# Moving list numbers and two blocks of gate products to GpSimd, and one block of one-hots to VectorE, in a two-phase attention and product-key expert kernel

## The reference

```python
q = (x @ Wq + bq).reshape(B, S, 8, 64)              # 8 heads
s1 = einsum(q[..., :32], K1); s2 = einsum(q[..., 32:], K2)   # 64 scores each
v1, i1 = top_k(s1, 10); v2, i2 = top_k(s2, 10)
all_scores = v1[..., :, None] + v2[..., None, :]
all_indices = i1[..., :, None] * 64 + i2[..., None, :]
vals, best = top_k(all_scores, 10)                   # 80 (head, place) slots a token
expert_idx = take_along_axis(all_indices, best)
h = gelu(einsum(x, W_down[expert_idx])) * softmax(vals)
out = einsum(h, W_up[expert_idx])
```

## Time and profile before

| what | value |
|---|---|
| time before, median of 3 | 3576.75 us (3570.31 to 3582.39) |
| the profiled execution's own time | 3578.76 us |
| its span from first to last instruction | 3577.0 us |
| PE busy | 89% |
| DVE busy | 87% |
| ACT busy | 59% |
| POOL busy | 53% |
| mean granted clock of PE | 0.887 of full |

### The profile page before, as it was taken

One profiled execution on the slowest core, in us unless ns is written; L12 is line 12 of the kernel. 1 busy time (PEld: TensorE's weight loads), 2 busy tenths in 40 slices (PEclk: granted clock), 3 DMA queues, 4 the chain that ended last, 5 costly groups with the idle time before them and its releaser, 6 DMA issues. The chain is left out here.

```text
span 3577.0 us, 91251 instructions
## 1 busy us (share of the span) xinstructions
PE 3185.3 (89%) x31284; PEld 2739.2 (77%) x31284; DVE 3098.0 (87%) x15084; ACT 2120.2 (59%) x4411; POOL 1901.8 (53%) x1694
## 2 busy tenths in 40 slices
PE   5999999963599999999999999999999999999988
PEld 3666666642488888888888888888888888888878
DVE  5666666646999999999999999999999999999971
ACT  3444444422666666666666766666666666766662
POOL 1333333333466665556556666666555555666664
PEclk9999999985699889888888988998998888988988
DMA  2111111103333333333333333333333333333332
GB/s 64 48 54 54 54 54 53 42 30 135 137 118 119 112 105 119 116 105 105 105 105 120 124 119 118 118 106 104 126 110 105 105 105 113 124 123 117 113 115 96
DMA packets 132329, 356.85 MB, mean 100 GB/s; under 512 B 13866, under 2 KB 61610, under 8 KB 129453
## 3 DMA queue, kind: packets, MB, share of 16 engines
q1 hardware_dynamic: 131868, 351.03, 30.0%
HBM read 309.01 MB, written 25.17 MB: 93 GB/s over the span
## 5 line engine op out<-in xcount | busy, mean ns | idle before, releaser
L1196 PE MATMUL b_ps_a<-b_wup,b_hid 128*128 128x256 f32 x4096 | 955.8, 379 | 1.5 <-POOL b_hid L1020 1.5
L1185 PE MATMUL b_ps_h<-b_xT_hi,b_wd_split 128*128 128x256 f32 x4096 | 934.4, 312 | 21.3 <-ACT b_hid L1336 20.5
L1196 PEld LDWEIGHTS b_ps_a<-b_wup,b_hid 128*128 128x128 f32 x4096 | 744.3, 190 | 85.7 <-POOL b_hid L1020 1.7
L1020 POOL TENSOR_TENSOR b_hid<-b_hid,b_gates 128x512 f32<-128x512 f32 x512 | 662.2, 1296 | 228.8 <-ACT b_hid L1336 228.8
L1185 PEld LDWEIGHTS b_ps_h<-b_xT_hi,b_wd_split 128*128 128x128 f32 x4096 | 705.5, 201 | 37.0 <-issue 26.5
L1315 ACT ACTIVATE b_ohq<-b_q_no,b_minus_qid 80x128 f16<-80x128 f16 x2048 | 648.7, 391 | 1.0
L1110 PE MATMUL b_ps_s<-b_ohr,b_ohq 80*128 80x32 f16 x16384 | 452.9, 185 | 173.5 <-issue 132.2
L1001 POOL TENSOR_SCALAR b_rstd<-b_mv 128x2 f32<-128x2 f32 x64 | 140.6, 2197 | 870.6 <-DVE b_mv L1375 870.6
L1185 PE MATMUL b_ps_h<-b_xT_lo,b_wd_split 128*128 128x256 f32 x2048 | 597.8, 292 | 0.0
L1110 PEld LDWEIGHTS b_ps_s<-b_ohr,b_ohq 80*128 80x128 f16 x16384 | 444.2, 102 | 182.4 <-issue 138.9
L1336 ACT ACTIVATE b_hid<-b_ps_h 128x512 f32<-128x512 f32 x512 | 303.9, 594 | 373.0 <-PE b_ps_h L1185 372.9
(11 more groups left out here) (192 smaller groups left out, 5534.4 us busy)
## 6 DMA issues: line engine op xcount, KB each, us to landing
b_wd_split<-wd_parts SPq DMA_DIRECT2D x512, 512.0 KB, 3.8
a_keysh<-a_key SPq DMA_DIRECT2D x16, 896.0 KB, 5.4
a_x<-in_x SPq DMA_DIRECT2D x16, 512.0 KB, 5.0
x_between<-a_y SPq DMA_DIRECT2D x16, 512.0 KB, 3.2
b_x<-x_between SPq DMA_DIRECT2D x32, 256.0 KB, 2.8
wd_parts<-b_wd_split SPq DMA_DIRECT2D x16, 512.0 KB, 3.1
b_x1t<-x_between SPq DMA_DIRECT2D x32, 256.0 KB, 5.4
out<-b_y SPq DMA_DIRECT2D x32, 256.0 KB, 5.5
```

Source lines behind the costliest of these rows:

```text
L1020: G.tensor_tensor(hid[:, p % 4, :, :], hid[:, p % 4, :, :], gates[:, 2 * p:2 * p + 2, :], ALU.mult).then_inc(mix_done, 1)
L1185: mm = T.matmul(hbank[p % 2][:, j * C:(j + 1) * C], a, c, start=i == 0, stop=i == len(parts) - 1)
L1196: mm = T.matmul(abank[:, t * D:(t + 1) * D], hid[:, p % 4, j, t * P:(t + 1) * P], wup[:, 2 * p + j, :], start=p == 0 and j == 0 and t == 0 ...
```

## The change

Four things change together.

1. `numbers` is moved from DVE to POOL, ahead of `pair_numbers` at place 10.
2. POOL no longer makes block 0 of `ohq`. It multiplies blocks 0 and 1 of `ohr` by the high and low gates, 10 parts of 13 tokens at places 3 to 12 (AT_PARTS), two instructions a part with a wait between them. DVE makes the equality of both blocks in one instruction (`equal`), between `lists_first` and `lists_rest`.
3. ACT makes block 0 of `ohq` instead of block 1, and DVE makes blocks 1, 2 and 3. The factors for POOL's one-hots go from `decode`. `ohq` now has three buffers and `ohr` all four blocks; block 3 of `ohq` shares the buffer of block 0 and waits for PE to have read that one.
4. `low_gates` moves from place 5 to 3; the places found by the second top-k lie in the memory of `picked`; ACT's `r_numbers` and `negate` come ahead of the first gelu.

```diff
-POOL_PARTS = 13
+POOL_PARTS = 10
+AT_PARTS = 3
-AT_GLO, AT_CID = 5, 10
+AT_GLO, AT_CID = 3, 10
-    ohq = sb("b_ohq", [SLOTS, C, NQ], F16)
-    ohr = sb("b_ohr", [SLOTS, 2, BLK, 2, NR], F16)
+    ohq = sb("b_ohq", [SLOTS, 3, BLK, NQ], F16)
+    ohr = sb("b_ohr", [SLOTS, C, 2, NR], F16)
...
-        def onehots(m, p):
...
-            G.tensor_tensor(ohq[:, tok, :].rearrange("p n (a b) -> p n a b", a=16),
-                            oh16[:, tok, :].unsqueeze(3).to_broadcast(shape),
-                            oh8[:, tok, :].unsqueeze(2).to_broadcast(shape), ALU.mult).then_inc(ohq_pool_done, 1)
+        def onehots(m, i):
+            tok = slice(i * 13, min(i * 13 + 13, 2 * BLK))
+            shape = [SLOTS, tok.stop - tok.start, NR]
+            hi, lo = (ohr[:, tok, part, :] for part in range(2))
+            pool.wait_ge(equal_done, m + 1)
+            pool.wait_ge(glo_done, m + 1)
+            G.tensor_tensor(hi, lo, ghi[:, tok, 0:1].to_broadcast(shape), ALU.mult).then_inc(pool_hi_done, 1)
+            pool.wait_ge(pool_hi_done, POOL_PARTS * m + i + 1)
+            G.tensor_tensor(lo, lo, glo[:, tok, 0:1].to_broadcast(shape), ALU.mult).then_inc(pool_lo_done, 1)
...
+        def numbers(m):
+            i = idx[:, :, :, 0:TOPK].rearrange("p t (h s) k -> p h s k t", s=2)
+            pool.wait_ge(lists_done[0], 5 * (m + 1))
+            pool.wait_ge(lists_done[1], 5 * (m + 1))
+            if m:
+                pool.wait_ge(cid_done, m)
+            G.tensor_scalar(id1[:, :, :, :], i[:, :, 0, :, :], float(NSQ), -2048.0, ALU.mult, ALU.add)
+            G.tensor_scalar(id2[:, :, :, :], i[:, :, 1, :, :], 0.0, None, ALU.add).then_inc(ids_done, 1)
...
                 if p == AT_CID and has(m + 2):
+                    numbers(m + 2)
                     pair_numbers(m + 2)
-                if p < POOL_PARTS and has(m + 1):
-                    onehots(m + 1, p)
+                if p >= AT_PARTS and p < AT_PARTS + POOL_PARTS and has(m + 1):
+                    onehots(m + 1, p - AT_PARTS)
...
+        def equal(m):
+            shape = [SLOTS, 2 * BLK, NR // 2, 2]
+            dve.wait_ge(q_no_done, 1)
+            dve.wait_ge(rid_done, m + 1)
+            if m:
+                dve.wait_ge(gates_pe, GROUPS * m)
+            V.tensor_tensor(ohr[:, 0:2 * BLK, 1, :].rearrange("p n (r s) -> p n r s", s=2),
+                            rid[:, 0:2 * BLK, :].unsqueeze(2).to_broadcast(shape),
+                            q_no[0:SLOTS, 0:NR].rearrange("p (r s) -> p r s", s=2).unsqueeze(1).to_broadcast(shape),
+                            ALU.is_equal).then_inc(equal_done, 1)
...
             if has(m + 2):
                 lists_first(m + 2, 0)
+            if has(m + 1):
+                equal(m + 1)
...
-                numbers(m + 2)
                 pair_sums(m + 2)
...
-                onehots_r(m + 1, 0)
+                onehots_r(m + 1, 2)
             if has(m + 1):
-                onehots_r(m + 1, 1)
+                onehots_q(m + 1, 1)
                 onehots_q(m + 1, 2)
             if has(m):
                 finish(m)
             if has(m + 1):
-                onehots_q(m + 1, 3)
-                onehots_r(m + 1, 2)
+                onehots_r(m + 1, 3)
             if has(m):
                 norm_out(m)
             if has(m + 1):
-                onehots_r(m + 1, 3)
+                onehots_q(m + 1, 3)
```

More of the change, by code:

```diff
@@ L826, in experts_phase @@
     idx = sb("b_idx", [P, NT, LISTS, 16], U16)
-    top, pos = val[:, 0, :, :], idx[:, 0, :, :]
+    top = val[:, 0, :, :]
     id1 = sb("b_id1", [P, HEADS, TOPK, NT], F16)
@@ L878, in experts_phase @@
     half_set, xT_lo_done, wd_lo_done, mix_done, res_done = (sem(f"b_{n}") for n in ("half", "xT_lo", "wd_lo", "mix", "res"))
-    ohq_pool_done, cid_done, glo_done = (sem(f"b_{n}") for n in ("ohq_pool", "cid", "glo"))
+    pool_hi_done, pool_lo_done, cid_done, glo_done = (sem(f"b_{n}") for n in ("pool_hi", "pool_lo", "cid", "glo"))
     eps_done = [sem(f"b_eps{i}") for i in range(2)]
@@ L889, in experts_phase @@
     shift_done, gsum_done, grecip_done, gate_done = (sem(f"b_{n}") for n in ("shift", "gsum", "grecip", "gate"))
-    q_no_done, eid_done, fields_done, qid_done, id16_done, oh16_done = (
-        sem(f"b_{n}") for n in ("q_no", "eid", "fields", "qid", "id16", "oh16"))
+    q_no_done, eid_done, fields_done, qid_done, equal_done = (
+        sem(f"b_{n}") for n in ("q_no", "eid", "fields", "qid", "equal"))
     ohr_eq_done, ohr_hi_done, ohr_lo_done, ohq_done = (sem(f"b_{n}") for n in ("ohr_eq", "ohr_hi", "ohr_lo", "ohq"))
@@ L1109, in gate_matrix @@
                     for part in range(2):
-                        mm = T.matmul(bank[:, n * NR:(n + 1) * NR], ohq[:, tok, :], ohr[:, b % 2, tok - b * BLK, part, :],
+                        mm = T.matmul(bank[:, n * NR:(n + 1) * NR], ohq[:, b % 3, tok - b * BLK, :], ohr[:, tok, part, :],
                                       start=part == 0, stop=part == 1)
@@ L1314, in distances @@
             for i in range(p * n, (p + 1) * n):
-                op = S.activation(ohq[:, BLK + i, :], q_no[0:SLOTS, :], ACT.Abs, bias=minus_qid[:, i:i + 1])
+                op = S.activation(ohq[:, 0, i, :], q_no[0:SLOTS, :], ACT.Abs, bias=minus_qid[:, i:i + 1])
             op.then_inc(distance_done, 1)
@@ L1319, in near @@
             n = BLK // ACT_PARTS
-            rows = ohq[:, BLK + part * n:BLK + (part + 1) * n, :]
+            rows = ohq[:, 0, part * n:(part + 1) * n, :]
             act.wait_ge(distance_done, PAIRS_R * m + (part + 1) * PAIRS_R // ACT_PARTS)
@@ L1344, in act_program @@
                     turn_gates(m + 1)
+                if p == 0 and has(m + 1):
+                    r_numbers(m + 1)
+                    negate(m + 1)
                 if has(m):
@@ L1347, in act_program @@
                 if has(m + 1):
-                    if p == 0:
-                        r_numbers(m + 1)
-                        negate(m + 1)
                     distances(m + 1, p)
@@ L1382, in onehots_q @@
             dve.wait_ge(qid_done, m + 1)
-            if m:
+            if b == BLOCKS - 1:
+                dve.wait_ge(gates_pe, GROUPS * m + BLOCK_GROUPS)
+            elif m:
                 dve.wait_ge(gates_pe, GROUPS * m)
-            V.tensor_tensor(ohq[:, tok, :].rearrange("p n (q s) -> p n q s", s=2),
+            V.tensor_tensor(ohq[:, b % 3, :, :].rearrange("p n (q s) -> p n q s", s=2),
                             qid[:, tok, :].unsqueeze(2).to_broadcast(shape),
@@ L1391, in onehots_r @@
             tok = slice(b * BLK, (b + 1) * BLK)
-            n = BLOCKS * m + b
+            n = 2 * m + b - 2
             dve.wait_ge(q_no_done, 1)
             dve.wait_ge(rid_done, m + 1)
-            if n >= 2:
-                dve.wait_ge(gates_pe, BLOCK_GROUPS * (n - 1))
+            if m:
+                dve.wait_ge(gates_pe, GROUPS * m)
             shape = [SLOTS, BLK, NR // 2, 2]
-            hi, lo = (ohr[:, b % 2, :, part, :].rearrange("p n (r s) -> p n r s", s=2) for part in range(2))
+            hi, lo = (ohr[:, tok, part, :].rearrange("p n (r s) -> p n r s", s=2) for part in range(2))
             V.tensor_tensor(lo, rid[:, tok, :].unsqueeze(2).to_broadcast(shape),
@@ L1421, in decode @@
             if m:
-                dve.wait_ge(ohq_done, 2 * m)
+                dve.wait_ge(ohq_done, 3 * m)
                 dve.wait_ge(minus_qid_done, m)
[L1424 to L1439, removed]
+            V.scalar_tensor_tensor(qid[:, :, :], twice(eid[:, 2, :]), float(NSQ), twice(eid[:, 1, :]), ALU.mult,
+                                   ALU.add).then_inc(qid_done, 1)
         def finish(m):
```

47 lines of the change are left out of this document (16 added, 31 removed).

## The result

The changed kernel takes 3589.56 us (median of 8 runs, 3583.95 to 3595.36), the kernel before 3575.07 in the same series: ratio 1.0039, 95% interval 1.0028 to 1.0049. It is slower by 14.5 us, where I had forecast 57, and it lies 5 us under the forecast's own range of 3595 to 3690. The profiled execution has a span of 3589.9 us, 12.9 more than before.

A forecast was written before the change was run, and what follows sets the result against it. DVE was taken as the bound at 82.7 us a chunk; 73.6 without port waits plus 11.0 of waits made 84.6, 1.9 more, and 30 turns of that 57 us: about 3634 us, range 3595 to 3690.

The forecast's parts named there:

- DVE without port waits: DVE's list for one chunk after the change, summed without waits for the port shared with POOL: 73.6 us.
- wait at `equal`: DVE's joint equality meets POOL's add_input or the pause before mix 1: 0.6 us of port wait a chunk.
- waits at the pair sums: DVE's five pair sums stand in POOL's dense stream and wait for the port: 5.8 us a chunk, between 4.4 and 10.
- shift and copies: DVE's shift and position copies get through only when POOL's stream ends: 4.0 us of port wait a chunk.
- root steps: The root steps between DVE's remaining one-hots cost 0.6 us of port wait a chunk.
- end of POOL's stream after the decode: POOL's last mix ends at about 54.6 us after the decode, against 49.9 before the change.
- PE waits for mixes: PE waits in `up` for POOL's later mixes, some 3 us a chunk.
- PE waits for the last `ohq` block: PE's gate matrix of block 3 waits some 4 us a chunk for DVE's one-hots.
- Port waits that come: New waits on DVE's list for the port held by POOL: 0.6 + 5.8 + 4.0 + 0.6 = 11.0 us a chunk.
- Rival 1: Pair sums and copies slip in at POOL's pauses, under 9 us of port waits a chunk: 3514 us, chance 0.28.
- Rival 2: A wash: DVE's port waits between 8.7 and 9.5 us a chunk, 3566 to 3588 us, chance 0.13.
- Rival 3: Each DVE pair sum loses twice, or POOL's products take 1.0 us instead of 0.84: 3727 us, chance 0.10.

The follow-up runs named there:

- e5: The changed kernel with 16 more MAX8 on DVE ahead of the pair sums, 2.1 us a chunk: 3596.86 us.
- e9: The changed kernel with one 432-element pair sum for five, and DVE waiting for POOL's last mix ahead of shift and copies: 3604.4 us.
- e10: The changed kernel with DVE waiting for POOL's last mix ahead of the shift and position copies, nothing else: 3596.03 us.
- e7: The changed kernel with `low_gates` done twice on POOL, 1.25 us more of its stream in each chunk: 3616.2 us.
- e3: The changed kernel with `numbers` and the pair numbers moved behind POOL's last mix: 3562.56 us.
- e2: The changed kernel with `numbers` back on DVE, between the lists and the pair sums: 3554.18 us.
- e6: The changed kernel with one pair-sum instruction of 432 elements in place of five, leaving out the right pairing: 3687.22 us.
- e1: The kernel before with only `numbers` moved to POOL and the places found kept in the memory of `picked`: 3563.92 us.
- e4: The changed kernel with the two position copies on ACT instead of DVE: 3576.86 us.

## Why the prediction was wrong

The direction, the places of the new waits and POOL's course came as forecast; the size did not: 84.6 us a chunk were forecast, 83.1 measured, +57 us against +14.5. By its steps:

| step, us a chunk | forecast | measured in the chunk shown |
|---|---|---|
| DVE without port waits | 73.6 | 83.3 - 10.0 = 73.3 |
| wait at `equal` | 0.6 | 3.23 - 2.3 = 0.9 |
| waits at the pair sums | 5.8 | 5.47 - 0.85 = 4.6 |
| shift and copies | 4.0 | 5.08 - 0.59 = 4.5 |
| root steps | 0.6 | 0 |
| end of POOL's stream after the decode | 54.6 | 2095.93 - 2041.54 = 54.4 |
| a part of products, two with the wait | 1.82 | 1.80 |
| `numbers` on POOL | 1.4 | 1.15 |
| PE waits for mixes | 3 | 2.0 |
| PE waits for the last `ohq` block | 4 | 2.9 |

Here 5.47 and 5.08 run from the first start of the group to the start of what follows (2079.57, 2096.15). What is taken off them is the instructions' own time: 2.3 and 0.85 are the prediction's estimates, 0.59 is the same stretch before (2089.14 to 2089.73).

**The step that failed** is "Port waits that come", and in it the sum 0.6 + 5.8 + 4.0 + 0.6 = 11.0 along DVE's list. The paragraph itself says that the copies get through only when POOL's stream ends, near 54.6. From there the chunk is settled by what DVE does behind the copies, and that could have been had from the trace of before: from the mask to the next decode it takes

```profile
2089.73 2.41 DVE L1556 TENSOR_TENSOR b_score<-b_posf,b_pair_no 128x4320 f16<-128x4320 f16 x1
...
2121.39 0.39 DVE L1412 TENSOR_SCALAR b_eid<-b_ps_m 80x256 uint16<-80x256 f32 x1
```

31.7 us; two r blocks of three instructions (3.64 each, L1399 at 2094.50 to L1399 at 2098.14) leave and an `ohq` block of 4.33 start to start comes, 28.7. The trace after has 2124.86 - 2096.15 = 28.7. So 54.6 and 28.7 make 83.3 us, +0.6 on the mean chunk, some +20 us, with no more knowledge than the prediction had (+1.0, 30 us, on the chunk of before that these rows show, 82.3). That 83.3 is met to the tenth is luck: 54.6 is 0.2 too late, and the sum leaves out the 0.2 us by which the mask starts behind POOL's end. My list gave 84.6, 1.5 above the measured mean: 0.6 for root steps that cost DVE nothing (it is POOL that waits there, 1.09 and 1.68 us for instructions of 0.22 and 0.71 alone), 0.4 for the three waits ahead of the mask (10.4 against 10.0), 0.3 in the sum without waits, and 0.2 by which the mean chunk is under the one shown. Each is small; thirty times 1.5 is 45 us, three times the effect.

**The uncertainty stood in the wrong place.** The waits at the pair sums, 4.4 to 10 us, made most of my range and the condition of two rivals. But while DVE arrives at the copies ahead of POOL's end, a us more there is a us less at the copies, and the chunk stays. It came out 1.2 lower and the tail 0.5 higher. e5 shows it from one side (2.1 us more ahead of the copies cost 0.2), e9 against e10 from the other (3.9 less gained nothing). What the chunk does hang on is POOL's stream, as e7, e3 and e2 show: +1.25 us there +1.0, `numbers` away -1.2.

**What the gain came to.** The change does take 9.4 us off DVE's list (82.7 to 73.3), and 10.0 us of port waits came in their place (9.9 in the mean chunk, which makes the 0.44). POOL's stream ends 4.5 us later after the decode (54.4 against 49.9), and so the mask starts 4.0 later (54.6 against 2089.73 - 2039.12 = 50.6), while what stands behind it is only 3.0 shorter (28.7 against 31.7). The chunk shown is 1.0 longer, the mean chunk 0.44. The waits decide nothing by themselves; in the change the work that was taken from DVE's first half was worth nothing, and that taken from its second half less than what POOL got.

**The rivals.** Rival 1 (lighter waits, 3514) had its premise fail, 10.0 us of waits and not under 9, and its reasoning too: in e6 the pair sum and the copies get in at POOL's pauses, just as it says, and the kernel is 3% slower than before, since DVE's mask and product then come early too. Rival 2's time ended at 3588, just under the result, but for another reason than its own (waits of 8.7 to 9.5 us). Rival 3 (products at 1.0 us) did not come: 0.96 + 0.84 start to start.

**Two pages beside the rows.** The GPSIMD Engine Reference of the Trainium skill (Elementwise — side-by-side cycle accounting) counts 2.6 cycles an element for two inputs; with the 1.2 GHz of the same section that is an estimate of 2.17 ns an element, 0.90 us for 416 without a start (the prediction put the whole product at 1.06 and shows no working for it). The trace has 0.84 to 0.96 start to start, and between 352 and 416 elements (0.78 and 0.89 us) 1.7 ns an element, so the measurement decides. The page SBUF — State Buffer of the Trainium skill (Who interferes with whom) says that whoever issues first has the pair for a whole instruction; e6 shows it in the direction that I had not priced, POOL's products at 3.05 us behind DVE's 2.4 us mask. That a waiting instruction is passed over several times is in these traces beside it (L1518 in e1, 6.4 us).

**What stays open.** Whether POOL's next instruction wins because it is queued without a pause, or for another reason, was not measured by itself; that pauses let DVE in rests on e2 and e6. Why the first phase differs by up to 9 us between the profiled executions was not followed up. Items 2 to 4 of the change were not tried one by one, so the 22 us of e2 belong to them together.

## What to carry to other kernels

When two engines share a port and one of them runs a dense stream, do not add up waits along the other's list: find the point where the list meets the end of the stream, and sum from there (the stream up to its end, then the list behind it). Two edits that each spend the same slack are priced together, not one by one; here -12 and -22 made +14.5. And an engine that comes early to a shared port is not free: hold it back, or place its long instructions where the critical engine's stream has ended.

## What the runs showed of the hardware

- A blocked DVE instruction shows its wait as busy time, not idle: a `tensor_scalar` of 160 elements 6.3 us for some 0.23 us of work before, a two-input sum of 64 elements 2.14 us, two strided copies of 80 two-byte elements of 0.2 us each 4.6 us after.
- The wait passes to whichever instruction stands there next: L1496 (6.3 us) before, the first pair sum in e1 (6.4 us), shift or mask in e2, e4, e5 and e7.
- Where POOL pauses for 0.09 us at its own semaphore DVE gets in: `numbers` on DVE waited 6 us behind POOL's stream without such pauses, 1.2 us with them (e2).
- Once in, DVE delays POOL by its whole instruction: products of 0.89 us took 3.05 and 2.93 (e6), a mix of 1.27 took 3.25 beside `equal`.
- A two-input f16 product of 416 elements on POOL takes 0.84 us start to start and 0.96 with its semaphore wait; `tensor_scalar` from uint16 to f16, 160 elements, 0.35 and 0.66 us.
